# Output blocks placed between the conditioned products of a step, with ScalarE's and VectorE's order to match

## What is computed

```python
c = einsum('bsi,boi->bso', x, w2[ids])        # conditioned 1024 x 1024 product, one of 16 weights per sequence
out = c @ W.T + b                             # FFN product
scores = c @ gate_w.T + gate_b                # gate over 4 ranks (8, 16, 32, 64)
probs = softmax(scores); sel = top-1 of probs; weight = probs[sel] / probs[sel]
out += weight * ((c @ A[:rank].T) @ B[:, :rank].T)     # low-rank part of the selected rank
x = x + out
```

## Time and profile before

| | before |
|---|---|
| median of 3 runs | 2372.76 us |
| the profiled execution's own time | 2369.65 us |
| its span | 2368.0 us |
| TensorE matmul busy | 2306.8 us (97%) |
| VectorE busy | 1242.3 us (52%) |
| ScalarE busy | 956.5 us (40%) |
| mean granted TensorE clock | 0.993 |
| conditioned products, L1229 and L1231 | 627.7 and 406.6 us |
| output blocks, L1258 and L1260 | 485.9 and 265.4 us |

### The profile page before, as it was taken

How to read it: one execution, slowest core, us unless ns; L and a number is a source line. 1 busy time by engine, 2 the same in 40 slices (tenths; PEclk the granted TensorE clock), 3 DMA queues, 4 the chain that set the end, 5 groups by cost and what they waited for, 6 DMA issues and landing times.

```text
span 2368.0 us, 73775 instructions
## 1 busy us (share of the span) xinstructions
PE 2306.8 (97%) x28506; PEld 1730.6 (73%) x28506; DVE 1242.3 (52%) x3466; ACT 956.5 (40%) x2459; POOL 38.5 (2%) x84
## 2 busy tenths in 40 slices
PE   7899999999999689999999999999999999999998
PEld 4677777777777478787878787878787878787775
DVE  7677777777777554343334343433344334433443
ACT  5577777777777432222222222222222222222221
POOL 0000000000000000000000000000000000000000
PEclk9999999999999999999999999999999999999999
DMA  7766767677777732141213141214215132231302
GB/s 271 289 244 253 279 249 282 248 288 255 273 269 261 272 115 109 38 144 37 81 64 140 41 147 70 71 40 141 75 65 187 37 108 79 102 108 37 126 20 107
DMA packets 108927, 356.45 MB, mean 151 GB/s; under 512 B 27568, under 2 KB 28720, under 8 KB 79152
## 3 DMA queue, kind: packets, MB, share of 16 engines
q1 hardware_dynamic: 97872, 280.89, 32.8%
q0 software_dynamic: 9792, 71.31, 8.0%
q10 hardware_dynamic: 1056, 1.05, 0.1%
HBM read 218.99 MB, written 134.22 MB: 149 GB/s over the span
## 4 chain that ended last, share of the span: by engine, by line
PE 93%; DMA 3%; DVE 2%; SPq 1%; issue 1%; ACT 1%; DVEq 0%
PE bank L1258 20%; PE bank L1229 19%; PE bank L1127 19%; PE bank L1231 10%; PE bank L1260 9%; PE bank L1084 3%; PE bank L1086 3%; PE bank L1085 3%; PE bank L1268 2%; DMA stage<-w_in 2%; PE bank L1240 1%; PE bank L1267 1%; DVE wf L834 1%; DMA xr<-x 1%; PE bank L1242 1%
## 5 line engine op out<-in xcount | busy, mean ns | idle before, releaser
L1229 PE MATMUL bank<-xs,w 128*128 128x128 f16 x8192 | 627.7, 220 | 23.0 <-DVE xs L841 23.0
L1127 PE MATMUL bank<-w,xs 128*128 128x384 f16 x3072 | 557.8, 329 | 5.0 <-DVE w L854 5.0
L1229 PEld LDWEIGHTS bank<-xs,w 128*128 128x128 f16 x8192 | 474.7, 98 | 30.8 <-issue 23.5
L1258 PE MATMUL bank<-y,wf 128*128 128x512 f16 x2048 | 485.9, 380 | 0.6 <-DVE xr L886 0.6
L672 ACT ACTIVATE zh<-bank 128x256 f32<-128x256 f32 x256 | 98.2, 384 | 825.9 <-PE bank L1231 823.0
L1127 PEld LDWEIGHTS bank<-w,xs 128*128 128x128 f16 x3072 | 291.8, 99 | 167.4 <-issue 5.9
L1231 PE MATMUL bank<-xs,w 128*128 128x64 f16 x8192 | 406.6, 193 | 0.0
L882 DVE SCALAR_TENSOR_TENSOR xr<-bank,xr 128x256 f32 (+1 forms) x256 | 108.7, 425 | 478.8 <-PE bank L1268 416.7
L1231 PEld LDWEIGHTS bank<-xs,w 128*128 128x128 f16 x8192 | 336.6, 98 | 0.0
L1258 PEld LDWEIGHTS bank<-y,wf 128*128 128x128 f16 x2048 | 181.2, 98 | 205.0 <-DVE xr L886 0.8
L1260 PE MATMUL bank<-y,wf 128*128 128x256 f16 x2048 | 265.4, 273 | 0.0
(11 more groups left out here) (156 smaller groups left out, 2070.0 us busy)
## 6 DMA issues: line engine op xcount, KB each, us to landing
stage<-w_in SPq DMA_DIRECT2D x68, 1024.0 KB, 8.9
w<-ws POOLq DMA_DIRECT2D x68, 1024.0 KB, 6.1
ws<-wf SPq DMA_DIRECT2D x64, 1024.0 KB, 6.6
xr<-x SPq DMA_DIRECT2D x128, 256.0 KB, 3.5
out<-xr SPq DMA_DIRECT2D x128, 256.0 KB, 2.4
xr<-x_in SPq DMA_DIRECT2D x31, 1024.0 KB, 8.0
x<-xr SPq DMA_DIRECT2D x31, 1024.0 KB, 4.4
wcf<-wc_in SPq DMA_DIRECT2D x128, 32.0 KB, 4.5
```

What stands on the lines that cost most here:

```text
L1127: e = mm(zps[q % 2][h][:, 0:384], lhs, rhs[:, k, h * 384:(h + 1) * 384], start=(k == 0 and lhs is a and rhs is wq_h), stop=(k == K - 1 and ...
L1229: mm(both, hi[:, k, c], x_k, start=(k == 0), stop=False)
L1258: mm(fps[m % 2][:, :], wf_h[:, k, c], yhl[:, u, k, :], start=(k == 0), stop=False)
```

## The change

TensorE's `b_step` no longer makes four output blocks behind the fourth set. In a j = 1 step block 4 stands ahead of set 1, block 5 ahead of set 2, block 6 ahead of set 3 and block 7 behind set 3. In a j = 0 step the transposes and blocks 0 and 1 stand behind set 2, ahead of set 3, and blocks 2 and 3 behind set 3. VectorE's `residual` calls are spread in the same way. On ScalarE all four `out_chunks` of a step move up, from the end of the step to the place behind `gate_copy` and `gate_exp` and ahead of `y_set` 1; `middle_copy` moves ahead of `y_set` 3. The work is the same, instruction for instruction. The code behind the steps (the last group) is unchanged. The whole diff:

```diff
@@ ScalarE, b_step @@
                 if j == 0 and before:
                     gate_exp(pi, pu)
+                if before:
+                    out_chunks(pi, pu, range(4 * j, 4 * j + 4), phase_b=True)
                 if first and q < 2:
...
                     x_hi(i, q + 1, phase_b=True)
                 y_set(i, q, 2)
-                y_set(i, q, 3)
                 if j == 0 and before:
                     middle_copy(pi, pu)
-                if before:
-                    out_chunks(pi, pu, range(4 * j, 4 * j + 4), phase_b=True)
+                y_set(i, q, 3)
@@ VectorE, b_step @@
                     unit_lo(IA, 2 * q, range(NPC), 2 * q)
+                if before and j == 1:
+                    residual(pi, pu, [4], phase_b=True)
                 y_set(i, q, 1)
...
                         x_lo(i, q + 1, b, phase_b=True)
+                if before and j == 1:
+                    residual(pi, pu, [5], phase_b=True)
                 y_set(i, q, 2)
+                if before:
+                    residual(pi, pu, [0, 1] if j == 0 else [6], phase_b=True)
                 y_set(i, q, 3)
                 if before:
-                    residual(pi, pu, range(4 * j, 4 * j + 4), phase_b=True)
+                    residual(pi, pu, [2, 3] if j == 0 else [7], phase_b=True)
@@ TensorE, b_step @@
                 for t in range(1, TS):
+                    if before and j == 1:
+                        ffn(pi, pu, [3 + t])
                     cond_set(i, q, t, need)
-                if j == 0 and before:
-                    transposes(pi, pu)
+                    if before and j == 0 and t == 2:
+                        transposes(pi, pu)
+                        ffn(pi, pu, [0, 1])
                 if before:
-                    ffn(pi, pu, range(4 * j, 4 * j + 4))
+                    ffn(pi, pu, [2, 3] if j == 0 else [7])
```

## The result

The changed kernel took 2516.02 us (median of 4 runs, 2512.68 to 2520.69), against 2372.35 us for the kernel before on the same chip. The ratio is 1.0608, 95% interval 1.059 to 1.0625: 143.7 us more. The forecast was 2472 us with a range of 2455 to 2545 us. The range holds the result, the likeliest case (2469 to 2480 us) doesn't: the predicted wait is there in its predicted size, and the second rival, a clock that falls in the wait, came true in two waits of three (20 of 31).

What follows compares the result with a forecast made beforehand. TensorE, busy throughout the steps, was taken as the bound. Waits of 1.66 + 1.45 + 0.10 = 3.21 us in 31 j = 0 steps add 99.5 us to 2369.65: 2469.2, forecast 2472 us as median, range 2455 to 2545 us.

Steps and rivals of the forecast that it cites:

- the likeliest case: Whole kernel: new waits of 3.21 us in 31 j = 0 steps, forecast 2472 us (ends 2469 and 2480), chance 0.74.
- the second rival: TensorE's clock falls to half rate behind each new wait, adding 31 x 2.3 = 71 us: 2543 us, chance 0.13.
- No gain possible: TensorE, steps with output blocks: busy for 1468.20 of 1468.20 us, so a new order has no idle time to win.
- The transposes one set earlier: TensorE, j = 0: transposes come up 2.72 us earlier with 1.06 us to spare, so they wait 1.66 us for `mhl`.
- a handover: TensorE's start behind the end of VectorE's releasing instruction, j = 0: taken as 0.10 us, between 0.06 and 0.23.
- The chunks, 1.45 us: ScalarE, j = 0: four bias chunks ahead of `y_set` 1 delay `zh` and so `mhl` by 1.45 us (1.39 to 1.57).
- `mT`: ScalarE's copy for L1267 in j = 0 steps: ready 0.5 us in time, nothing added, next one to be late.
- j = 1, gate, DMA: Blocks between sets in j = 1 steps, the next step's gate, and weight loads on DMA queues: all cost nothing.
- The clock: TensorE: granted clock expected to stay at 1.00 behind waits of 3.2 us, nearer the 2.22 us case than 6.35 us.
- falls in each wait: Rival: half-rate TensorE work behind every new wait costs about 2.3 us each, 71 us in all; chance 0.13.
- falls in none: The forecast's own case: clock stays at 1.00 behind all 31 waits, 2472 us; chance 0.74.
- the rival with 0.13: The clock falling behind each new TensorE wait: 71 us added, 2543 us, chance 0.13.

Runs made afterwards that it cites:

- e6: Changed kernel with VectorE's gating 2 ahead of `y_set` 1 instead of behind it in j = 0 steps: 2423.37 us, ratio 1.0213.
- e3: Changed kernel with j = 0 steps put back as in the kernel before on all three engines, j = 1 steps as changed: 2371.43 us, ratio 0.9997.
- e4: Changed kernel with 16 matmuls, result unread, put ahead of the transposes in each j = 0 step: 2473.07 us, ratio 1.042.
- e5: Changed kernel with two of a j = 0 step's four chunks ahead of `y_set` 1 and two behind the copy of `mT`: 2485.78 us, ratio 1.0473.

## Why the prediction was right, and where its likeliest case failed

*No gain possible: right.* With all waits gone the new order gives 0.9997 (j = 1 alone) and 1.0004 (both) of the time before.

*The transposes one set earlier, 1.66 us and a handover: right.* Alone they cost 1.72 us a step.

*The chunks, 1.45 us: right place, size at the upper end.* L1032 was 1.54 us later. The first chunk started 1652.25 - 1651.94 = 0.31 us behind the exponential, not 0.12, so nothing overlapped there; my row for the handover, the chunks behind `mT`, was of another instruction, 0.36 us long and not 0.21 (whether the length is the reason was not tried). The handover to TensorE made up for it: 1658.07 - 1658.01 = 0.06 us, the lower end. The sum, 3.21 us, was measured as 3.23 us on average: 100.2 us in the 31 waits against 99.5.

*`mT`: right.* No step waited for it: for L1273 at 1609.90 us it was copied from 1609.01 to 1609.38, 0.52 us in time, where 0.5 was worked out. It was the next one to be late, as e6 shows, where the transposes no longer wait.

*j = 1, gate, DMA: right.* e3 shows it for the j = 1 steps, and the changed kernel's list of waits has no entry for the gate or for a load of weights.

*The clock: the step that failed.* I set the new wait between one idle time of 2.22 us without a fall and one of 6.35 us with one, and took it for nearer to the short one. I gave "falls in each wait" 0.13 and "falls in none" 0.74; it fell in 20 of 31, a case that was not among my rivals. The row of 2.22 us was one draw, and not a typical one. The same place at the start of phase B, with a wait of 1.98 to 2.22 us, stands in all nine profiles; the clock fell behind it in six of them and stayed at 1.00 in the kernel before, e4 and e5. In the changed kernel, where the same wait was 2.18 us (its timeline row, then the granted clock behind it):

```profile
848.08 1.01 PE L1235 MATMUL bank<-xs,w 128*128 128x128 f16 x8 [2.18 <-DVE xs L841]
```
```profile
848.50:850.00 1.50, 1.50 (x21) 1.50 (x20) 0.89 (x3) 0.80 (x3) 0.00 (x0) 0.50 0.98 399
```

In the steps there are 31 waits a run: no fall with waits of 1.7 us, 22 with waits of 2.4 us, 20 with waits of 3.2 us, and none with waits as long in which TensorE worked for 1.7 us. The price per fall was about right: 2.1 us against 2.3 us from the earlier trace rows. With the clock at 20 of 31 the sum would have been 2472 + 20 x 2.3 = 2518 us. That the range holds 2516 us is owed to its upper end, which the rival with 0.13 had set; the forecast itself is 44 us short, nearly all of it by this one term.

The Trainium skill (TensorE: Matmul & The Clock Gate, section HAM oscillation — how this bites in real kernels) describes a kernel that pays for a cold engine again behind every wait between bursts. The trace agrees in kind, and not in "every": 11 of 31 waits left the clock alone, and waits of 2.4 us brought as many falls as waits of 3.2 us.

## What to carry to other kernels

Where one engine is busy all the time, ask of each moved block not what it hides but what it was hiding: here one set of products covered a chain through two other engines with 1 us to spare, and it was moved behind that chain's end, while four harmless instructions on an engine with time to spare moved into the chain. A wait of a few microseconds that returned every step had two prices on TensorE here, 100 us for its length and some 42 us for a slower clock behind it; count the second for part of the waits even if a single wait of that length in the trace went without. To interleave without a wait, move the links of the chain up with its consumer.

## What the runs showed of the hardware that I had not expected

Falls of the clock don't follow the length of the wait alone: in the same kernel, with waits of 3.13 and 3.35 us, the clock fell to 0.50 behind some and stayed at 1.00 behind others, and a fall could come in the wait (0.83 over the wait at 1654.7 us) or only when matmuls were running again (1540.64 us in e5). And 1.74 us of matmuls whose result nobody needs, put into a wait, made the kernel 43 us faster. What decides a single fall was not tried; that in e5 three steps of four have one, in a fixed order, speaks for something with a rhythm of its own, and is no proof of it.
